# A recurrent layer on one NeuronCore: decay product behind the mixes, bonus sums behind the gather, centring behind the keys, first scans right behind the first products

## What is computed

```python
xa = _ln(x, ln1_w, ln1_b)
sx = jnp.concatenate([state[:, 1:2] - xa[:, :1], xa[:, :-1] - xa[:, 1:]], axis=1)
xxx = jnp.tanh((xa + sx * maa_x) @ maa_w1).reshape(b, l, 5, DM)
xxx = jnp.einsum('blfd,fde->blfe', xxx, maa_w2)
xm = xa[:, :, None] + sx[:, :, None] * (maa_stack + xxx)
xk, xw, xv, xr, xg = (xm[:, :, j] for j in range(5))
w = jnp.exp(-jnp.exp(time_decay + jnp.tanh(xw @ td_w1) @ td_w2)).reshape(b, l, h, s_)
...
def step(s, rkvw):
    r_t, k_t, v_t, w_t = rkvw
    a = k_t[..., :, None] * v_t[..., None, :]
    out = jnp.einsum('bhi,bhij->bhj', r_t, u * a + s)
    s = a + w_t[..., :, None] * s
    return (s, out)
...
x1 = x + og * g @ Wo.T
```

## Time and profile before

| | |
|---|---|
| three runs | 981.23, 982.72, 985.28 us; median 982.72 |
| span of the profiled execution | 982.8 us, granted TensorE clock 0.995 on average |
| busy: PE | 944.6 us (96%) |
| busy: DVE | 592.1 us (60%) |
| busy: ACT | 462.5 us (47%) |
| busy: POOL | 411.8 us (42%) |
| chain that ended last | PE 74%, DVE 12%, ACT 5% |

### The profile page before, as it was taken

The page is one execution under the profiler, slowest core; times in us unless marked ns, Lnnn a source line. Parts: engine busy times, 40 slices in busy tenths (PEclk is TensorE's granted clock), DMA queues, the critical chain, the costliest instruction groups (busy, mean ns, idle before and its releaser), DMA issues.

```text
span 982.8 us, 21494 instructions
## 1 busy us (share of the span) xinstructions
PE 944.6 (96%) x8321; PEld 795.7 (81%) x8321; DVE 592.1 (60%) x974; ACT 462.5 (47%) x1026; POOL 411.8 (42%) x572
## 2 busy tenths in 40 slices
PE   6999999989999999999999999999999999999998
PEld 4777777966788888988897888998888888678776
DVE  5899986767544433344356433344426766999883
ACT  4677874237643333333334333333342434576565
POOL 2143346875365333333246343342422862344231
PEclk9999999999999999999999999999999999999999
DMA  9100000310011110111101110111100100000000
GB/s 298 37 23 2 2 2 22 116 54 2 1 55 50 54 50 25 37 54 48 54 7 55 50 54 21 42 49 48 54 22 18 41 14 1 1 2 6 13 6 23
DMA packets 24147, 37.15 MB, mean 38 GB/s; under 512 B 4432, under 2 KB 16528, under 8 KB 23824
## 3 DMA queue, kind: packets, MB, share of 16 engines
q1 hardware_dynamic: 24080, 36.23, 11.9%
HBM read 35.17 MB, written 1.05 MB: 37 GB/s over the span
## 4 chain that ended last, share of the span: by engine, by line
PE 74%; DVE 12%; ACT 5%; issue 4%; POOL 4%; DMA 0%; DVEq 0%; ACTq 0%; POOLq 0%
PE ps L1292 18%; PE ps L790 13%; PE ps L1309 9%; PE ps L1351 6%; PE ps L1948 5%; PE ps L890 4%; PE ps L1327 4%; PE ps L1337 2%; DVE sb L2476 2%; DVE sb L656 1%; PE ps L270 1%; DVE sb L650 1%; PE ps L2026 1%; PE ps L421 1%; PE ps L2112 1%
## 5 line engine op out<-in xcount | busy, mean ns | idle before, releaser
L837 POOL TENSOR_TENSOR sb<-sb 128x256 fp32r<-128x256 f32 (+1 forms) x128 | 102.5, 801 | 278.0 <-DMA sb<-in_heads_a 144.9
L1292 PE MATMUL ps<-sb 128*128 128x512 f32 x768 | 187.7, 396 | 1.0 <-issue 1.0
L1292 PEld LDWEIGHTS ps<-sb 128*128 128x128 f32 x768 | 139.5, 188 | 33.0 <-ACT sb L1425 3.1
L790 PE MATMUL ps<-sb 128*128 128x256 f32 x1152 | 148.4, 286 | 0.0
L790 PEld LDWEIGHTS ps<-sb 128*128 128x128 f32 x1152 | 141.4, 191 | 2.1 <-issue 0.2
L839 POOL TENSOR_TENSOR sb<-sb 128x256 fp32r<-128x256 f32 (+1 forms) x128 | 115.8, 905 | 10.0
L1522 DVE SCALAR_TENSOR_TENSOR sb<-ps,sb 128x512 fp32r<-128x512 f32 x64 | 45.1, 747 | 95.6 <-ACT sb L1458 95.5
L1309 PE MATMUL ps<-sb 128*128 128x256 f32 x768 | 99.2, 285 | 0.4 <-DVE sb L1490 0.4
L1502 DVE TENSOR_REDUCE sb<-ps 128x8 f32<-128x520 f32 x32 | 22.4, 700 | 126.6 <-PE ps L1327 126.6
L1309 PEld LDWEIGHTS ps<-sb 128*128 128x128 f32 x768 | 95.0, 191 | 3.0 <-issue 0.9
L1425 ACT ACTIVATE sb<-ps,sb 128x512 f32<-128x512 f32 x64 | 43.8, 685 | 107.9 <-PE ps L1292 107.8
(11 more groups left out here) (221 smaller groups left out, 1668.2 us busy)
## 6 DMA issues: line engine op xcount, KB each, us to landing
sb<-in_heads_a SPq DMA_DIRECT2D x32, 386.0 KB, 3.0
sb<-in_heads_c SPq DMA_DIRECT2D x16, 256.0 KB, 3.6
sb<-in_heads_b SPq DMA_DIRECT2D x32, 128.0 KB, 3.1
sb<-in_mlp_a SPq DMA_DIRECT2D x16, 128.5 KB, 2.1
sb<-in_mlp_b SPq DMA_DIRECT2D x16, 128.0 KB, 2.1
sb<-in_w_r SPq DMA_DIRECT2D x1, 2048.0 KB, 7.5
sb<-in_encT SPq DMA_DIRECT2D x1, 1024.0 KB, 6.2
sb<-in_ctx SPq DMA_DIRECT2D x1, 1024.0 KB, 8.1
```

The source lines that it names most:

```text
L790: last = pe.matmul(m.acc(t), lhsT[x], rhs[w], start=opens and n == 0, stop=False, skip_group_check=True)
L837: pool.tensor_tensor(high, src, one, ALU.mult).then_inc(*G.did(name + "_high", u))
L1292: last = pe.matmul(m.ps[u][:, c, :], m.w_parts[u][w][:, (KD * q + k) * P:(KD * q + k + 1) * P], rows[x][:, k, c * 512:(c + 1) * 512], star ...
```

## The change

Nothing is computed otherwise; instructions stand in another order, and one wait becomes narrower. (Three lines fewer above them move the later lines of the file by one.)

```diff
         pe.wait_ge(*done["ruk"].at(i))
         if i >= 1:
             pe.wait_ge(*done["x1"].at(i - 1))
-        for e in range(KD):
-            pe.matmul(m.c0[:, D + e * P:D + (e + 1) * P], m.headsum_u[:, e, :], m.ruk[i % 2][:, e * P:(e + 1) * P],
-                      start=True, stop=True)
         pe.wait_ge(*done["rs0"].at(i))
         pe.wait_ge(*done["rs1"].at(i))
         for jh in range(2):
             for jl in range(4):
-                last = pe.matmul(m.c0[jl * 32:(jl + 1) * 32, 0:D], m.gather[:, jh, :], m.sc[:, 2 * jl + jh, :],
-                                 start=jh == 0, stop=jh == 1)
+                pe.matmul(m.c0[jl * 32:(jl + 1) * 32, 0:D], m.gather[:, jh, :], m.sc[:, 2 * jl + jh, :],
+                          start=jh == 0, stop=jh == 1)
+        for e in range(KD):
+            last = pe.matmul(m.c0[:, D + e * P:D + (e + 1) * P], m.headsum_u[:, e, :], m.ruk[i % 2][:, e * P:(e + 1) * P],
+                             start=True, stop=True)
         last.then_inc(*done["o"].did(i))
...
-        decay2(slot - 2)
         spread1(slot - 2)
+        ffn_keys(slot - 5)
         center(slot - 3)
-        ffn_keys(slot - 5)
         ffn_receive(slot - 5)
...
         mixes(slot)
+        decay2(slot - 1)
         if slot == 0:
             fc2(pe, ph, m, 1, 1, 3)
         spread0(slot - 1)
     gather(LAST - 1)
-    decay2(LAST)
     spread1(LAST)
...
         f_stats(slot - 4)
+        decay2(slot - 2)
         if slot:
             a_stats(slot + 1)
         rows(slot)
...
-        decay2(slot - 2)
         f_normed(slot - 4)
...
         vec.wait_ge(*done["av0"].at(i))
-        vec.wait_ge(*done["av1"].at(i))
+        if part:
+            vec.wait_ge(*done["av1"].at(i))
...
         products0(slot - 5)
+        scan0(slot - 5)
         bonus(slot - 6)
         out_heads(slot - 6)
+        products1(slot - 5)
         mix2(slot - 4)
...
-        products1(slot - 5)
         group_sum(slot - 6)
...
-        scan0(slot - 5)
         group_rstd(slot - 6)
```

## The result

| | before | after |
|---|---|---|
| median of 5 runs | 982.92 us (981.23 to 987.69) | 1000.08 us (998.42 to 1001.64) |
| ratio | 1 | 1.0165 [1.0144, 1.0185] |
| profiled span, mean granted clock | 982.8 us, 0.995 | 996.6 us, 0.988 |

The account below looks back on a forecast made before the run. TensorE's queue was taken to bound the full slots, and the longer ring through project the fill after the change. 982.8 us plus 10.7 for order and 2.5 for clock gave 996.0 us, own range 991 to 1001, with the late-state rival 988 to 1002.

Parts of the forecast that it names:

- The start state is late: First scans wait last for GpSimd's copy of the start state, 4.4 us after the end of the mixes.
- the rival: Start state not late, a_stats running sooner in ScalarE's idle time: order sum 6.7 us, 989.5 us; 8 in 100.
- The three distances: End of mixes to project's first matmul, first three slots of the pipeline's fill: longer by 4.2, 2.0 and 3.5 us.
- The 0.7 us of mix2 against GpSimd's receive: In tile 0's slot, mix2 waits 0.7 us because GpSimd's receive is still reading; included in that slot's +4.2.
- The full slots: Mixes to project after the first three slots: -0.3 us in the fourth, +0.6 in tile 4's, 0 for tiles 5 to 7.
- The drain: Pipeline's end: +0.25 us from the moved decay product and +0.64 from bonus sums behind the gather, together 0.9.
- ffn_keys ahead of center, 0: On TensorE, keys cover center's later wait for og except 0.8 us in tile 4's slot, already counted; no extra cost.
- Sum of the order: All reordering terms together: +10.9 us, taken as +10.7 for fewer changes of shape on TensorE.
- project to the end of the mixes: The other half of each slot's ring, from project's first matmul to the mixes' end; claimed not touched by the change.
- TensorE's clock: Half-clock falls behind new TensorE waits in the fill: 1.5 falls of 1.67 us, +2.5 us, bounds 0 to 5.0.
- The case with three falls: Clock falls at each long TensorE gap, +5.0 us, 998.5 us; 2 in 10 within the forecast.
- Faster, through the freed meetings: Second scans no longer meet GpSimd's receive, freeing 5.8 us of VectorE's queue in the fill: 977.9 us; 7 in 100.

Follow-up runs that it names:

- e3: The changed kernel with GpSimd's copy of the start state put ahead of f_rstd, a_state and a_rstd; 998.0 us, ratio 1.0124.
- e6: The kernel before with the decay product alone moved, behind the mixes on TensorE and ahead of a_stats on ScalarE; 985.01 us, ratio 1.0011.
- e10: The kernel before with the bonus sums behind the gather, nothing else, one run; 985.44 us beside 985.21.
- e5: The kernel before with ffn_keys ahead of center in the full slots, nothing else moved; 989.38 us, ratio 1.0056.
- e4: The changed kernel with 46 more keep-warm matmuls where TensorE would stand idle in the fill; 993.38 us, ratio 1.0102.
- e8: The kernel before with VectorE doing GpSimd's receive itself for tiles 0 to 2, order unchanged; 983.68 us, ratio 0.9993.

## Why the prediction was right, and which term was too small

996.0 us were forecast, 1000.1 measured, within 988 to 1002. By its steps:

- **The start state is late.** Right. L2650 released the scans in four slots; 4.4 us from the mixes to the first scan were forecast, 4.2 measured, and 5.4 against 5.3 in the slot where f_stats stands ahead too. e3 takes the wait away and gets back 1.35, 0.3 and 1.6 us, where the working of the rival had 1.5, 0.3 and 1.6; the rival itself (989.5 us) falls. (The decay product's 0.64 is 0.61 in the row that it names and in after, which changes nothing.)
- **The three distances**, +4.2, +2.0 and +3.5: measured +4.1, +1.9, +3.4. The 0.7 us of mix2 against GpSimd's receive are there too: 2.21 us for 1.48, the receive running from 828.62 to 830.42. The Trainium skill, "SBUF — State Buffer", "Who interferes with whom", has VectorE instructions with two SBUF inputs contend with a GpSimd instruction that reads SBUF; the row agrees: 0.73 us longer for 0.87 us beside the receive. What the prediction adds from there, that an instruction with at most one SBUF input does not contend, the page limits to instructions outside VectorE's 2-port modes.
- **The full slots**, -0.3, +0.6 and 0: measured -0.3, +0.6, then -0.3 and -0.15, which may be the fewer changes of shape that I had put at up to 0.4 in all. e6 and e10 each show 0.15 to 0.2 a slot for a changed place of the same matmuls; that the shapes are the reason is not shown.
- **The drain**, +0.9: measured +0.8; e10 shows 0.6 for the bonus sums alone.
- **ffn_keys ahead of center, 0.** Right for this change, and in part by luck: the cover that I named (1.9 us of keys against 0.8) was not the whole of it. e5 shows that the same move costs 5.4 us when VectorE's queue is the old one. I had looked at who waits at center and not at what stands behind group_sum on VectorE.
- **Sum of the order**, +10.7: e4 measured +10.7. That it fits to the tenth is luck: I had said that project to the end of the mixes isn't touched, and it grew by 0.5 us in one slot (attended's wait in e4), while the last full slots gave back about as much.
- **TensorE's clock, +2.5 (0 to 5.0). This is the term that was mis-sized**: 6.3 us, above its upper bound. I took 1.5 falls of 1.67 us; there were three, of 2.5, 2.9 and 1.0 us. The price was wrong since I had it from two groups of 24 matmuls and a window of 4 us; in after half clock lasts some 7 us each time. The case with three falls, to which I gave 2 in 10 and 998.5 us, was the one that came. The Trainium skill, "TensorE: Matmul & The Clock Gate", "HAM oscillation — how this bites in real kernels", has the clock throttled anew at each wait between bursts of matmuls; the windows of after agree, 0.52, 0.57 and 0.52 granted at the three places with waits, so the page spoke for the three-fall case. Its example has waits of 3 to 5 us, though, and the second fall here came with 1.85 and 1.10 us.
- **Faster, through the freed meetings**: falls. It needed the three distances to grow by less than 5 us together, and they grew by 9.4. The second scans do take 3.0 us in after. I had summed the freed meetings to 5.8 us with 1.4 for the eight scans; e8 has 2.1 there (6.82 to 4.76). What the whole of that time would be worth in the old order no run tells, since e8 gave a part of it back to VectorE as its own receive: it got 0.8 us.

What stays open: how the second fall comes about. It follows on 1.85 and 1.10 us of idle time with 0.7 us of centring and some other work between, 1.4 us in all, where before 1.02 us were borne; e4 filled all waits at once, so no run tells which gap did it.

## What to carry to other kernels

When a step is moved forward in a queue, count the waits that it brings, not its own duration: 1.8 us of scans brought a chain over four engines, and 2 to 4 us a slot of the fill. Where the moved waits leave TensorE idle between products, price the clock as its own term, one fall for each long wait; here a fall cost 1.0 to 2.9 us; keep-warm matmuls in the gap test this, and gave back 6.3 of 17.0 us. And try the parts singly before believing any of them harmless: here VectorE's part alone cost 37 us and the keys' alone 5, and all parts together 17.

## What the runs showed that I had not expected

- Half clock came in long stretches: 0.52 to 0.57 granted over 7 to 8 us behind waits of 1.85 to 3.85 us, though TensorE was busy for most of them (5.17 of 7.00 us in the first).
- The order of the same matmuls has a price of its own. With decay product or bonus sums in another place a full slot got 0.15 to 0.2 us shorter (e6, e10), though TensorE had the same work and waited for nothing in it before or after; the reason stays open.
- The scan of VectorE pays for GpSimd's reads too: eight in 4.76 us with GpSimd's receive away and 6.82 beside it, five in 3.01 (after) or 3.49 (e8) and in 5.13 (e5).
